# Leaving out the idle products of TensorE in the later stages of a one-core attention and expert kernel

## The chip, the cores and the metric

The kernel runs on one core of one Trainium2 chip. The metric is the device time of one execution in microseconds (us), lower is better. The times below are medians over separate executions; the profile is one further execution, taken by the hardware profiler.

## What is computed

One transformer layer on `x` of 1 x 256 x 512 (256 tokens, width 512), float32, in three steps, each a layer norm followed by a block whose result is added to `x`:

```
x = x + xattn(norm(x), ctx)     # 16 heads, 4096 context rows of width 128, rotary keys of width 64
x = x + attn(norm(x))           # causal latent attention, 16 heads, query/key width 96, value width 32
x = x + ffn(norm(x))            # 32 experts, 4 of them per token, capacity 10 tokens each, and a shared expert
```

The expert block: a router picks 4 of 32 experts for each token (first 3 of 8 groups, then 4 experts in them); each expert takes at most 10 tokens and computes `(silu(t @ W_gate) * (t @ W_up)) @ W_down` with 512 x 256, 512 x 256 and 256 x 512 weights; the results are weighted and added back to the tokens. A shared expert of inner width 512 is computed for all tokens.

## The kernel before

The program is written by hand for each engine, with semaphores. Each engine works through its own list in order. TensorE (PE) runs: a preparation stage (to about 60 us), the cross attention in 8 pairs of heads (to about 450 us), its output projection (to about 500 us), the second attention (`queries`, `scores2`, `transposes2`, `values2`, to about 546 us), the projection of its output into `x2_banks` (line 1287), the transposes of the normed tokens `xn_transposes(3)` (line 992), the router's logits (line 1295), and then the expert stage.

The expert stage, in TensorE's order: `shared_hidden(0)` (line 1307), which is the first quarter of the shared expert's hidden layer; the positions of the chosen tokens (lines 1324 to 1326), for which VectorE must have chosen the experts (`sel_done`); `chosen_rows(c)` (line 1335), which gathers the tokens of all experts by a product with a one-hot matrix that VectorE makes from the positions (`oh_done`); then eight groups of four experts, g = 0 to 7. For each group `gate_up(g, c)` runs for four quarters c of the width (line 1363), ScalarE and VectorE make silu(gate) * up, `hidden_back(g)` transposes it (line 1376), ScalarE copies it back, and `down(g)` (line 1397) multiplies by the down weights. Between them stand the other quarters of the shared expert, its output `shared_out` (line 1316) and `combine` (line 1406), which adds the experts' results into two accumulation banks. The last group has its down product in two halves n = 0, 1 of the output width, each followed by a copy on VectorE and `combine_last(n)` (line 1413); VectorE then adds to `x` (line 974) and two stores write the output.

The expert weights are 48 MB, 1.5 MB for an expert, and stream through a ring of 13 places of on-chip memory. SyncE (SP) issues the loads in a fixed order. Places 0 to 11 are filled before or during the second attention. The others are loaded when TensorE is through with what lay there: quarter by quarter for the first two groups (semaphore `gu_part`), then by expert. The last three experts (k = 29, 30, 31) are loaded last of all: their gate and up weights in four quarters (`ld_end_gu[c]`), then the down weights of group 7's first expert (k = 28), then the down weights of the last three in two halves (`ld_end_down[n]`, line 414). `down(6)` needs the down weights of k = 24 to 27; `down(7)` half n needs k = 28 and `ld_end_down[n]`.

TensorE's clock is granted at one of two levels. The kernel holds runs of idle products, made by `warm(n, bank)` at line 981: n products of a 128 x 128 by 128 x 512 bf16 matrix of constants into a bank whose content nobody reads. They compute nothing of the result. They stand in TensorE's list, so that work behind them waits for them.

Of the kernel before, what the change touches and what calls it, by code (L numbers as in the profile page):

```python
# [43 lines left out]
NG = E // GE  # L44
# [55 lines left out]
DVE_BEFORE = order("rows0 q0 rows1 rope0 rows2 q1 k0 rows3 q2 rope1 m0 k1 rope2 rope3 k2 m1 m2 q3 k3 m3 m4 m5 q4 k4 m6 m7 m8 q5 "  # L100
                   "k5 m9 m10 k6 m11 m12 q6 m13 k7 m14 m15 q7")
PAIR_BUFS = 6
WARM_START, WARM_HEADS, WARM_TURN, WARM_LAST, WARM_QUARTER, WARM_DOWN, WARM_CHOICE, WARM_ROWS = 14, 3, 4, 9, 3, 6, 3, 4


def expert(k):
# [12 lines left out]
def wait(eng, sem, value):  # L119

    if isinstance(value, int) and value <= 0:
        return
    eng.wait_ge(sem, value)
# [12 lines left out]
def layer(nc, a, out):  # L136
    with ExitStack() as ctx:
# [3 lines left out]
        def ps(name, cols):  # L141
            return ctx.enter_context(nc.psum_tensor(name, [P, cols], F32))
# [112 lines left out]
        psM = ps("psM", 1024)  # L255
        psA = [psM[:, 0:512], psM[:, 512:1024]]
        psE = [psS[0][:, 0:512], psS[0][:, 512:1024]]
        psF = [psS[1][:, 0:512], psS[1][:, 512:1024]]
# [719 lines left out]
        def _(pe):  # L978
            mm = nc.tensor.matmul

            def warm(n, bank, of=const[:, C_EARLY:C_EARLY + 256].bitcast(BF16)):

                for _ in range(n):
                    mm(bank[:, 0:512], of[:, 0:P], of[:, 0:512], start=True, stop=True)  # L984
# [3 lines left out]
            def xn_transposed(n, s):  # L988
                for c in range(DC):
                    if c % 2 == 0:  # L990
                        pe.wait_ge(ln_xn, 2 * (TT * (n - 1) + s) + c // 2 + 1)
                    last = nc.tensor.transpose(psE[s][:, P * c:P * c + P], xn[:, s, P * c:P * c + P], ident)
                last.then_inc(ln_tr, 1)

            def xn_transposes(n):
                for s in range(TT):
                    xn_transposed(n, s)
                    if n == 3 and s == 0:
                        warm(WARM_LAST, psF[1])

            def rope_transposes(n):
                pe.wait_ge(kr_done, n + 1)
# [178 lines left out]
            for h in range(H + 2):  # L1181
# [6 lines left out]
                if 1 <= h <= H:  # L1188
                    g = h - 1
# [31 lines left out]
            def values():  # L1221
                for st in range(TT):
                    mm(psF[st][:, :], ckv[:, P * st:P * st + P], w_vb, start=True, stop=True).then_inc(v_mm, 1)

            def queries(h):

                if h == 0:
                    pe.wait_ge(ld_qb, 16)
                if h % 4 == 0:
                    wait(pe, qk_copied, h)  # L1230
                    w = slice(NOPE * h, NOPE * (h + 4))
                    mm(psA[1][:, 0:T], w_qn[:, w], qa, start=True, stop=True)
                    mm(psA[1][:, T:2 * T], w_kn[:, w], ckv, start=True, stop=True).then_inc(nope_mm, 1)
                wait(pe, q2_turned, 2 * h - 2)
                mm(psE[h % 2][:, 0:T], w_qb[:, h, :], qa, start=True, stop=True).then_inc(q2_mm, 1)

            def scores2(h):
                if h == 0:
                    pe.wait_ge(kpe_spread, 1)
                    pe.wait_ge(v_copied, TT)  # L1240
                pe.wait_ge(q2_done, h + 1)
                pe.wait_ge(qk_copied, h + 1)
                wait(pe, s2_max, h - 1)
                q, k = qk[0:QW, h % QK_BUFS, 0:T], qk[0:QW, h % QK_BUFS, T:2 * T]
                mm(psF[h % 2][:, 0:P], q[:, 0:P], k[:, 0:P], start=True, stop=True)
                mm(psF[h % 2][:, P:3 * P], q[:, P:T], k, start=True, stop=True).then_inc(s2_mm, 1)

            def transposes2(h):
                pe.wait_ge(s2_exp, 2 * h + 2)
                wait(pe, pT_copied, h if h < NH2 - 1 else 0)  # L1250
                if h == NH2 - 1:
                    pe.wait_ge(qk_copied, NH2)
                for i in range(3):
                    last = nc.tensor.transpose(turned_bank(h)[:, P * i:P * i + P], sm[:, h % SM_BUFS, P * i:P * i + P], ident)
                last.then_inc(pT_mm, 1)

            def values2(h):
                pe.wait_ge(pT_copied, h + 1)
                w = slice(V2 * h, V2 * h + V2)
                mm(psO[0][:, w], pT[:, h % 2, 0:P], v2[:, 0, w], start=True, stop=True)  # L1260
                mm(psO[1][:, w], pT[:, h % 2, P:2 * P], v2[:, 0, w], start=True, stop=False)
                mm(psO[1][:, w], pT[:, h % 2, 2 * P:3 * P], v2[:, 1, w], start=False, stop=True).then_inc(o2_mm, 1)
            for h in range(NH2 + 5):
                if h < NH2:
                    queries(h)
                if h == 0:
                    values()
                if h in (2, 3):
                    warm(WARM_HEADS, psM[:, 0:512])
                if 0 <= h - 1 < NH2:  # L1270
                    scores2(h - 1)
                if 0 <= h - 3 < NH2:
                    transposes2(h - 3)
                if 0 <= h - 4 < NH2:
                    values2(h - 4)
            warm(WARM_TURN, psF[1])
            for st in range(TT):
                pe.wait_ge(o2_done, st + 1)
                for c in range(DC):
# [20 lines left out]
            def shared_hidden(i):  # L1300
                if i == 0:
                    pe.wait_ge(ld_shared[0], 16)
                elif i == DC - 1:
                    pe.wait_ge(sh_done, 2)
                for n in range(2):
                    for c in range(DC):
                        last = mm(sh_bank[i][:, T * n:T * n + T], sh_in[:, i, n, c, :], xnT[:, c, :], start=c == 0, stop=c == DC - 1)  # L1307
                last.then_inc(sh_mm, 1)
# [7 lines left out]
                        mm(psO[n][:, D // 2 * st:D // 2 * (st + 1)], hs[:, i, P * st:P * st + P], sd[:, i, halves[n]],  # L1316
                           start=i == 0 and st == 0, stop=False, skip_group_check=True)
            shared_hidden(0)
            warm(WARM_CHOICE, psF[1])
            pe.wait_ge(sel_done, 1)  # L1320
            pe.wait_ge(ld_const, 32)
            early, ones = const[:, C_EARLY:C_EARLY + P], const[:, C_ONES:C_ONES + P]
# [1 line left out]
            mm(psA[1][:, 0:E], early, chosen[:, 0, :], start=True, stop=True)  # L1324
            mm(psA[1][:, E:2 * E], ones, chosen[:, 0, :], start=True, stop=False)
            mm(psA[1][:, E:2 * E], early, chosen[:, 1, :], start=False, stop=True).then_inc(pos_mm, 1)
            warm(WARM_ROWS, psF[1])
            pe.wait_ge(cleared, 2)

            def chosen_rows(c):  # L1330
# [7 lines left out]
            def weights_by_slot():  # L1338
                pe.wait_ge(ow_done, 2 * TT)
                pe.wait_ge(hT_copied, 2)  # L1340
                for trio in range(TRIOS):
                    for st in range(TT):
                        o = T * trio + P * st
                        last = nc.tensor.transpose(psS[0][:, o:o + P], ow[:, st, P * trio:P * trio + P], ident)
                last.then_inc(back_mm, 1)
# [33 lines left out]
            def down(g):  # L1379
                trio = g // 3  # L1380
                pe.wait_ge(hT_copied, g + 1)
                wait(pe, y_copied, min(trio, TRIOS - 1))
                for j in range(GE):
                    k = GE * g + j
                    if k < ENDING:
                        pe.wait_ge(ld_down[k % RING], 16 * (k // RING + 1))
                for n in range(2 if trio == TRIOS - 1 else 1):
                    if g == NG - 1 or g == NG - 2 and n == 0:
                        warm(WARM_DOWN, psF[0])
                    if g == NG - 1:  # L1390
                        pe.wait_ge(ld_end_down[n], 16 * (E - ENDING))
                    bank, out = (psA[n], slice(D // 2 * n, D // 2 * (n + 1))) if trio == TRIOS - 1 else (psA[trio % 2], slice(0, D))
                    for c in range(FC):
                        for j in range(GE):
                            k = GE * g + j
                            o = W_GU + D * c
                            last = mm(bank[SLOT * j:SLOT * j + SLOT, out], hT[:, g % 3, c, SLOT * j:SLOT * j + SLOT], ring[k % RING][:, o + out.start:o + out.stop],  # L1397
                                      start=g % 3 == 0 and c == 0, stop=(g % 3 == 2 or g == NG - 1) and c == FC - 1, skip_group_check=True)
                    if n == 1 or trio < TRIOS - 1 or g == NG - 1:
                        last.then_inc(y_mm, 1)  # L1400
# [29 lines left out]
            shared_hidden(2)  # L1430
            for g in range(2, NG):
                for c in range(DC):
                    if g == NG - 1:
                        warm(WARM_QUARTER, psF[0])
                    gate_up(g, c)
                if g == 2:
                    shared_hidden(3)
                    weights_by_slot()
                elif g < 3 + DC:
                    shared_out(g - 3)  # L1440
                if g == NG - 1:
                    down(g - 1)
                hidden_back(g)
                if g == 3:
                    combine(0)
                elif g == 6:
                    combine(1)
                if g != NG - 2:
                    down(g)
# [82 lines left out]
```

## Time and profile before

| | |
|---|---|
| median of 3 runs | 666.23 us (666.22 to 668.37) |
| profiled execution, its own time | 665.71 us |
| profiled execution, span of the instructions | 663.5 us |
| mean granted clock of TensorE in it | 0.995 |
| TensorE busy | 627.0 us (94%) |
| VectorE (DVE) / ScalarE (ACT) / GpSimd (POOL) busy | 389.3 / 363.0 / 178.1 us |
| read from device memory | 77.29 MB |

Times in the trace count from the span's start. The profiled execution's own time is 2.2 us above its span, and lies 0.5 us below the median. A row of the timeline gives start, duration, engine, line of the kernel, operation, output and inputs with their shapes, the number of instructions merged, and in square brackets how long the engine had been idle before and what released it. One float32 product appears as two instructions. Ends of matmuls are modelled, so that the last one of a row reaches a little into the next row, and a few records are missing. A granted clock of 1.00 is the upper level, 2.4 GHz; 0.50 is the lower, 1.2 GHz.

### The profile page before, as it was taken

To read this page: it belongs to the slowest core of one execution; us is meant where nothing else is said; L and a number is where in the kernel's file an instruction comes from. 1 tells how busy PE (TensorE), PEld (TensorE's weight loads), DVE (VectorE), ACT (ScalarE), POOL (GpSimd) and SP (SyncE) were. 2 spreads that over 40 slices of the span, in tenths; PEclk is the share of its full clock that TensorE was granted. 3 is DMA by queue.
4 is the path that set the end of the run, shared out by engine and by line. 5 is a ranking of instruction groups with operands and counts; after the bars stand their busy time and mean duration, and the time that the engine had idled before them with its cause. 6 is when DMAs were issued, how large, how long until landed. Compare 5 with 4: busy or idle time off the path is not lost.

```text
span 663.5 us, 15252 instructions
## 1 busy us (share of the span) xinstructions
PE 627.0 (94%) x5998; PEld 463.3 (70%) x6054; DVE 389.3 (59%) x549; ACT 363.0 (55%) x518; POOL 178.1 (27%) x143
## 2 busy tenths in 40 slices
PE   8999899999999999999999999999998999995997
PEld 5876766777777777777777778997556986361443
DVE  5979586767766766766766766553145865300001
ACT  4442765766776776776776777784126874100000
POOL 1260334444443443453453443000001320000000
PEclk9999999999999999999999999999999999997999
DMA  9953874224224224224224224204986043699993
GB/s 351 419 166 79 239 271 96 56 55 98 53 53 95 53 53 95 53 53 95 53 53 95 55 54 105 46 2 192 420 354 255 1 159 128 215 393 414 417 393 101
DMA packets 32152, 105.15 MB, mean 158 GB/s; under 512 B 4592, under 2 KB 9968, under 8 KB 27760
## 3 DMA queue, kind: packets, MB, share of 16 engines
q1 hardware_dynamic: 32112, 104.57, 49.6%
q8 instruction: 30, 0.49, 0.3%
q14 instruction: 10, 0.08, 0.0%
HBM read 77.29 MB, written 0.52 MB: 117 GB/s over the span
## 4 chain that ended last, share of the span: by engine, by line
PE 75%; DVE 9%; issue 6%; ACT 5%; DMA 3%; SPq 1%; POOL 1%; DVEq 0%; ACTq 0%
PE psO L1115 8%; PE psO L1124 8%; PE psO L1116 8%; PE psS L1102 7%; PE psS L1103 7%; PE psM L1074 5%; PE psS L1363 5%; PE psO L1180 4%; DMA arena<-rope 3%; PE psO L1059 3%; DVE arena L768 2%; PE psM L1397 2%; PE psO L1060 2%; PE psO L1307 2%; PE psS L984 1%
## 5 line engine op out<-in xcount | busy, mean ns | idle before, releaser
L768 DVE TENSOR_REDUCE arena<-psM 128x2 f32<-128x1024 f32 x121 | 147.7, 1221 | 66.6 <-PE psM L1074 66.2
L589 ACT ACTIVATE arena<-psS 128x1024 bf16<-128x1024 f32 x128 | 131.3, 1026 | 88.9 <-PE psS L1103 86.8
L484 POOL TENSOR_TENSOR arena<-arena 128x1024 bf16<-128x1024 f32 x56 | 120.8, 2156 | 190.4 <-ACT arena L590 166.9
L1115 PE MATMUL psO<-arena 128*128 128x129 bf16 x1024 | 132.8, 220 | 1.5 <-ACT arena L589 1.2
L1116 PE MATMUL psO<-arena 128*128 128x128 bf16 x1024 | 132.4, 220 | 0.0
L590 ACT ACTIVATE arena<-psS 128x1024 f32<-128x1024 f32 x128 | 130.9, 1023 | 0.0
L1102 PE MATMUL psS<-arena 128*128 128x256 bf16 x512 | 120.5, 273 | 0.9 <-DVE arena L779 0.9
L1103 PE MATMUL psS<-arena 65*128 65x256 bf16 x512 | 120.8, 273 | 0.0
L1115 PEld LDWEIGHTS psO<-arena 128*128 128x128 bf16 x1024 | 99.1, 98 | 20.3 <-issue 12.7
L1116 PEld LDWEIGHTS psO<-arena 128*128 128x128 bf16 x1024 | 99.4, 97 | 6.7
L806 DVE TENSOR_TENSOR arena<-arena 128x1024 bf16<-128x1024 f32 x72 | 88.6, 1233 | 14.6 <-ACT arena L590 14.6
L1124 PE MATMUL psO<-arena 128*128 128x129 bf16 x1024 | 79.4, 220 | 0.7 <-DVE arena L806 0.5
L1124 PEld LDWEIGHTS psO<-arena 128*128 128x128 bf16 x1024 | 65.8, 97 | 3.5 <-DVE arena L806 1.8
L1102 PEld LDWEIGHTS psS<-arena 128*128 128x128 bf16 x512 | 50.2, 98 | 7.4 <-DVE arena L701 1.0
L1103 PEld LDWEIGHTS psS<-arena 65*128 65x128 bf16 x512 | 50.0, 98 | 5.4
L581 ACT CAST arena<-psO 128x512 bf16<-128x512 f32 x64 | 37.8, 591 | 26.6 <-PE psO L1060 26.6
L762 DVE TENSOR_TENSOR arena<-psO,arena 128x512 bf16<-128x512 f32 x64 | 43.8, 684 | 12.1 <-ACT arena L581 11.4
L1074 PE MATMUL psM<-arena 64*128 64x512 bf16 x242 | 47.1, 386 | 3.7 <-DVE arena L768 2.8
L1363 PE MATMUL psS<-arena 128*32 128x512 f32 x256 | 32.5, 638 | 5.8 <-issue 5.8
L960 DVE TENSOR_TENSOR arena<-psS,arena 128x256 f32<-128x256 f32 x8 | 3.4, 424 | 55.0 <-ACT arena L666 55.0
L1059 PE MATMUL psO<-arena 128*128 128x512 bf16 x64 | 24.3, 379 | 8.0 <-issue 7.5
L527 POOL TENSOR_TENSOR arena<-arena 64x256 f32<-64x256 f32 x16 | 11.5, 718 | 72.5 <-DVE arena L849 72.5
(197 smaller groups left out, 739.2 us busy)
## 6 DMA issues: line engine op xcount, KB each, us to landing
arena<-arena SPq DMA_DIRECT2D x96, 256.0 KB, 3.7
arena<-w_exp SPq DMA_DIRECT2D x20, 1024.0 KB, 16.0
arena<-w_exp SPq DMA_DIRECT2D x29, 512.0 KB, 13.4
arena<-w_exp SPq DMA_DIRECT2D x54, 256.0 KB, 8.1
arena<-w_pair SPq DMA_DIRECT2D x8, 1088.0 KB, 19.2
arena<-w_o SPq DMA_DIRECT2D x1, 4096.0 KB, 20.3
arena<-ctx SPq DMA_DIRECT2D x4, 512.0 KB, 12.8
arena<-rope SPq DMA_DIRECT2D x4, 512.0 KB, 14.1
```

Source lines behind the costliest of these rows:

```text
L484: nc.gpsimd.tensor_tensor(p_lo[:, s % 2, :], p_f[:, s % 2, :], p_hi[:, s % 2, :], ALU.subtract).then_inc(s_plo[0], 1)
L589: nc.scalar.activation(p_hi[:, s % 2, :], psS[s % 2][:, :], ACT.Exp).then_inc(s_phi, 1)
L590: nc.scalar.activation(p_f[:, s % 2, :], psS[s % 2][:, :], ACT.Exp).then_inc(s_pf, 1)
L768: nc.vector.reduce_max(maxes[:, :, st, c], maxima_bank(q, m)[:, :].rearrange("p (j n) -> p j n", j=2), AX.X).then_inc(s_mfree, 1)
L806: nc.vector.tensor_tensor(p_lo[:, s % 2, :], p_f[:, s % 2, :], p_hi[:, s % 2, :], ALU.subtract).then_inc(s_plo[s % 2], 1)
L1074: last = mm(bank[:, 512 * j:512 * j + 512], queries_of[r, P * st:P * st + P], k_hi[r, 512 * c:512 * c + 512], start=True, stop=True)
L1102: mm(o, k1[:, j, l], q1[:, j, :], start=True, stop=False)
L1103: last = mm(o, k2[0:R + 1, j, l], q2[0:R + 1, j, :], start=False, stop=True)
L1115: mm(psC[:, st, :], ph, vx[:, GROUP * g + i, 0:CW], start=g == 0 and i == 0 and st == 0, stop=False, skip_group_check=True)
L1116: last = mm(psC[:, st, 0:K], ph, vx[:, GROUP * g + i, CW:VW], start=False, stop=False, skip_group_check=True)
L1124: last = mm(psC[:, st, :], p_lo[:, s % 2, T * i + P * st:T * i + P * st + P], vx[:, GROUP * g + i, 0:CW], start=False, stop=g == HALF - 1 ...
L1363: last = mm(psF[g % 2][SLOT * j:SLOT * j + SLOT, :], xpT[:, c, CAP * e:CAP * e + SLOT], ring[k % RING][:, 2 * FI * c:2 * FI * (c + 1)], st ...
```

## The change

Of the eight constants that give the lengths of the idle runs only `WARM_START` (14 products in the first microseconds) is left; the seven others and their calls are deleted. That takes out of TensorE's list: 3 products each in the rounds h = 2 and 3 of the second attention, 4 after it, 9 between the two tiles' transposes of the third layer norm, 3 before the wait for the chosen experts, 4 after the positions, 3 before each of the four quarters of `gate_up(7, c)`, and 6 each before `down(6)`, `down(7)` half 0 and `down(7)` half 1. In all 56 products. Nothing is added or moved.

```
-WARM_START, WARM_HEADS, WARM_TURN, WARM_LAST, WARM_QUARTER, WARM_DOWN, WARM_CHOICE, WARM_ROWS = 14, 3, 4, 9, 3, 6, 3, 4
+WARM_START = 14
...
                     xn_transposed(n, s)
-                    if n == 3 and s == 0:
-                        warm(WARM_LAST, psF[1])
...
-                if h in (2, 3):
-                    warm(WARM_HEADS, psM[:, 0:512])
                 if 0 <= h - 1 < NH2:
                     scores2(h - 1)
...
-            warm(WARM_TURN, psF[1])
             for st in range(TT):
                 pe.wait_ge(o2_done, st + 1)
...
             shared_hidden(0)
-            warm(WARM_CHOICE, psF[1])
             pe.wait_ge(sel_done, 1)
...
-            warm(WARM_ROWS, psF[1])
             pe.wait_ge(cleared, 2)
...
                 for n in range(2 if trio == TRIOS - 1 else 1):
-                    if g == NG - 1 or g == NG - 2 and n == 0:
-                        warm(WARM_DOWN, psF[0])
                     if g == NG - 1:
                         pe.wait_ge(ld_end_down[n], 16 * (E - ENDING))
...
                 for c in range(DC):
-                    if g == NG - 1:
-                        warm(WARM_QUARTER, psF[0])
                     gate_up(g, c)
```

## Rows read from the trace of the kernel before

**Rows 1.** The page: granted clock and memory traffic, 40 equal slices of 16.6 us.
```profile
PEclk9999999999999999999999999999999999997999
GB/s 351 419 166 79 239 271 96 56 55 98 53 53 95 53 53 95 53 53 95 53 53 95 55 54 105 46 2 192 420 354 255 1 159 128 215 393 414 417 393 101
```

**Rows 2.** Timeline of TensorE after its longest idle time, and one group later.
```profile
607.77 6.10 PE L1363 MATMUL psS<-arena 128*32 128x512 f32 x32 [5.82 <-issue]
...
619.41 3.62 PE L1363 MATMUL psS<-arena 128*32 128x512 f32 x32
```

**Rows 3.** Timeline of all engines in the last 24 us.
```profile
640.64 1.89 PE L1406 MATMUL psO<-arena 128*128 128x256 f32 x8
...
643.11 1.06 PE L1363 MATMUL psS<-arena 128*32 128x512 f32 x8
...
649.90 0.42 DVE L960 TENSOR_TENSOR arena<-psS,arena 128x256 f32<-128x256 f32 x1 [10.34 <-ACT arena L666]
...
650.75 1.93 PE L1397 MATMUL psM<-arena 128*32 128x256 f32 x32
...
652.62 0.44 PE L1376 MATMUL psS<-arena 128*128 128x128 f32 x2
653.09 0.23 ACT L674 COPY arena<-psS 128x80 f32<-128x80 f32 x1 [3.22 <-PE psS L1376]
...
654.77 1.07 PE L1397 MATMUL psM<-arena 128*32 128x256 f32 x16
...
657.17 1.07 PE L1397 MATMUL psM<-arena 128*32 128x256 f32 x16
...
658.17 1.99 PE L1413 MATMUL psO<-arena 128*128 128x256 f32 x8
```

**Rows 4.** Two of the last loads: SP's issue, then KB and us from issue to landing.
```profile
637.52 2.81 SPq L414 DMA_DIRECT2D arena<-w_exp  x1
arena<-w_exp SPq DMA_DIRECT2D x1, 256.0 KB, 12.9
...
645.01 0.59 SPq L414 DMA_DIRECT2D arena<-w_exp  x1
arena<-w_exp SPq DMA_DIRECT2D x1, 256.0 KB, 7.4
```

**Rows 5.** Timeline of all engines, from the second attention's end to the logits.
```profile
545.95 1.29 DVE L875 TENSOR_TENSOR arena<-psO,arena 128x512 f32<-128x512 f32 x2 [1.75 <-PE psO L1262]
...
546.70 1.25 PE L1280 MATMUL psS<-arena 128*128 128x128 f32 x8
...
555.52 2.11 PE L984 MATMUL psS<-arena 128*128 128x512 bf16 x9
...
557.95 0.76 PE L992 MATMUL psS<-arena 128*128 128x128 f32 x4 [0.32 <-DVE arena L722]
```

**Rows 6.** Timeline of all engines, from the shared product to the gather.
```profile
560.29 3.70 PE L1307 MATMUL psS<-arena 128*128 128x256 f32 x16
...
564.99 0.41 PE L1324 MATMUL psM<-arena 128*128 128x32 f32 x2 [0.35 <-DVE arena L897]
...
565.98 0.89 DVE L933 TENSOR_TENSOR arena<-psM,arena 128x320 f32<-128x320 f32 x2 [0.33 <-PE psM L1326]
...
566.62 2.39 PE L1335 MATMUL psS<-arena 128*128 128x320 f32 x8
```

**Rows 7.** Timeline of all engines, start of the second attention.
```profile
509.91 0.30 PEld L1245 LDWEIGHTS psS<-arena 96*128 96x128 f32 x2 [0.61 <-POOL arena L527]
...
511.91 0.70 PE L1232 MATMUL psM<-arena 128*128 128x256 f32 x2 [0.75 <-ACT arena L630]
```

**Rows 8.** Windows: PE, PEld, DVE, ACT, POOL busy (instructions), granted clock, DMA share, GB/s.
```profile
598.00:600.00 2.00, 0.73 (x5) 0.28 (x3) 0.42 (x1) 1.11 (x3) 0.00 (x0) 1.00 1.03 412
...
605.50:606.00 0.50, 0.00 (x0) 0.00 (x0) 0.00 (x0) 0.00 (x0) 0.00 (x0) 0.94 1.06 397
...
612.50:613.00 0.50, 0.50 (x8) 0.14 (x4) 0.00 (x0) 0.00 (x0) 0.00 (x0) 0.73 0.99 410
```

More of the change, by code:

```diff
@@ L102 @@
 PAIR_BUFS = 6
-WARM_START, WARM_HEADS, WARM_TURN, WARM_LAST, WARM_QUARTER, WARM_DOWN, WARM_CHOICE, WARM_ROWS = 14, 3, 4, 9, 3, 6, 3, 4
+WARM_START = 14
 def expert(k):
@@ L997, in xn_transposes @@
                     xn_transposed(n, s)
-                    if n == 3 and s == 0:
-                        warm(WARM_LAST, psF[1])
             def rope_transposes(n):
@@ L1267, in _ @@
                     values()
-                if h in (2, 3):
-                    warm(WARM_HEADS, psM[:, 0:512])
                 if 0 <= h - 1 < NH2:
@@ L1275, in _ @@
                     values2(h - 4)
-            warm(WARM_TURN, psF[1])
             for st in range(TT):
@@ L1318, in _ @@
             shared_hidden(0)
-            warm(WARM_CHOICE, psF[1])
             pe.wait_ge(sel_done, 1)
@@ L1326, in _ @@
             mm(psA[1][:, E:2 * E], early, chosen[:, 1, :], start=False, stop=True).then_inc(pos_mm, 1)
-            warm(WARM_ROWS, psF[1])
             pe.wait_ge(cleared, 2)
@@ L1387, in down @@
                 for n in range(2 if trio == TRIOS - 1 else 1):
-                    if g == NG - 1 or g == NG - 2 and n == 0:
-                        warm(WARM_DOWN, psF[0])
                     if g == NG - 1:
@@ L1432, in _ @@
                 for c in range(DC):
-                    if g == NG - 1:
-                        warm(WARM_QUARTER, psF[0])
                     gate_up(g, c)
```

## The prediction

> **What bounds the kernel now.** I started with the page's slices [rows 1]. The clock is full throughout except near 605 us, and from 580 to 647 us memory traffic is at about 400 GB/s: the expert weights stream without a pause. Next, in the timeline of that stretch, I asked who waits for whom. TensorE waits 5.82 us for weights up to 607.77 [rows 2]; from there its work follows on to the end with waits of about half a microsecond at most. So in the last 56 us TensorE's own list sets the end, and the loads run ahead of it. The last look was at how far ahead: the last load, a piece of the second half of the last down weights, is issued at 645.01 and lands 7.4 us later, at 652.4; the product that needs it starts at 657.17 [rows 4, 3]. TensorE is 4.75 us late for its last weights. That distance decides this change, because the idle products of the last group lie in TensorE's list with no wait beside them that would cover them.
>
> The earlier idle products act on the end in another way. The weight stream restarts only when TensorE is through the first quarter products (about 570 us), and from 577 on the channel is full. A shift of TensorE's work before 570 shifts the whole stream, the end of the wait at 607.77 and the last landing by the same amount.
>
> **The change part by part.** 56 products go. A run of nine takes 2.1 us [rows 5]; below, pairs of starts give the cost of each run.
>
> *The last group (30 products).* Before, `gate_up(7)` starts at 643.11 and `down(6)` at 650.75, with three runs of 3 between the quarters and one of 6 behind: 7.64 us [rows 3]. The same 32 instructions take group 4, which has no idle products, 3.62 us [rows 2]. That part would shrink by 4.0 us. The run ahead of the first quarter reaches from the end of `combine`, 640.64 + 1.89 less the 0.07 by which a row's modelled end overlaps the next row (657.17 + 1.07 against 658.17), to 643.11: 0.65 us. The run before half 0 of `down(7)` reaches from the end of ScalarE's copy, 653.32, to 654.77: 1.4 us. Half 0 then takes 1.0 and half 1 starts at 657.17: another 1.4 us [rows 3]. TensorE's list loses 4.0 + 0.65 + 1.4 + 1.4 = 7.45 us.
>
> The end does not gain all of that, because the weights are late next. I follow the list without idle products. `gate_up(7)` runs from 642.46 to 646.08. `down(6)` takes 1.87 (650.75 to 652.62), to 647.95; VectorE's silu product of group 7 was ready 1.0 us after the last quarter (650.32 against 649.35) and is still covered by it. The transposes and ScalarE's copy take 0.7 (652.62 to 653.32), to about 648.7. Half 0 needs the load issued at 637.52 and landed 12.9 us later, at 650.4 [rows 4]: a wait of 1.7, which also hides a wait of `down(6)` for its own last weights. Half 0 ends at 651.4. Half 1 needs the last landing, 652.4, another wait of 1.0. The rest (half 1, `combine_last`, VectorE's add, the stores) follows half 1 as before. Gain: 657.17 - 652.4 = **4.75 us**. The other 2.7 us turn into waits for weights.
>
> *The runs of the routing stretch (9 + 3 + 4).* After the 9 products TensorE still waited 0.32 us for VectorE's norm (L722) [rows 5], after the 3 it waited 0.35 us for the chosen experts (L897) [rows 6]: both runs lie beside VectorE's work, gain 0. After the 4 the gather starts at 566.62. VectorE's two one-hot products take 0.89 us from 565.98: the first is there at 566.42, the second at 566.87 [rows 6]. The gather's second pair of instructions could start at about 567.0 where it started at 567.15: gain 0.15.
>
> *The 4 after the attention.* VectorE's first scaling ends at 545.95 + 0.65 = 546.6, the transposes start at 546.70 [rows 5]: gain 0.05.
>
> *The 3 + 3 in the attention.* About 0.65 us each, by the run ahead of the first quarter. Behind the second run TensorE waited for GpSimd's add, and at 511.91 it waits 0.75 us for ScalarE [rows 7]. Gain 0 therefore; the upper bound is 0.65, were TensorE to pace that stretch, the lower is nothing, since nothing there waits longer without them.
>
> Sum: 4.75 + 0.15 + 0.05 = 4.95 us. The profiled execution would take 665.71 - 4.95 = 660.8; the median lies 0.5 above it, so **661.3 us**, 0.74% faster.
>
> **What the clock may take back.** The idle products kept TensorE busy over stretches that now have holes, and the trace of before cannot show what the clock does there. It shows one fall. TensorE was idle from 601.95 to 607.77; the clock went to the lower level, 1.2 GHz, at about 606, after 4 us of idleness, and was back at 2.4 GHz at about 612.7, after 5 us of dense work [rows 8, 2]. The 32 instructions in it took 6.10 us where 3.62 are usual: 2.5 us is the price of one fall over dense work [rows 2]. The new holes are 2.4 us (555.5 to 557.95), 1.0 (to 564.99) and 0.6 in the routing stretch, and 1.7 and 1.0 at the end. All are shorter than the idleness that preceded the fall, and from 598 to 600 TensorE worked 0.73 of 2 us at full clock [rows 8]. So the main sum takes 0 for the clock (the bounds: 0, and both rivals below together, 5.4), and falls are priced as rivals. The fall at 606 itself stays; with TensorE 1.0 us early for its last weights, one costlier by up to 1.0 would be hidden.
>
> The Trainium skill, "TensorE: Matmul & The Clock Gate", section "A second HAM failure mode: psum-queue depth-cycling", says that many short pauses between groups of matmuls can be enough to make the clock go back and forth. By it the first two rivals would hold, one or both. No row here shows a fall of that kind.
>
> **The rivals.**
> *One: the clock falls in the routing stretch.* For it: the 2.4 us hole is followed by products with very small outputs and then by further holes. Against: none is as long as 5.82 us. Price: 2.5 us of slower dense work, mostly the shared product (3.70 us) [rows 6]. Up to 0.95 is hidden in the wait for the chosen experts, and up to 1.9 more is lost if the logits, for which VectorE waits, take twice their 1.9 us: 1.5 to 4.4, taken 2.5. The stream starts that much later: 663.8.
> *Two: the clock falls at the very end.* From 648.7 to 652.4 TensorE would work only 1.0 us. Price: half 1 and `combine_last`, 1.0 + 1.9 us, double [rows 3]: 2.9 us, 664.2. With the first together: 666.7, no change.
> *Three: the loads do not hold TensorE up.* If the last landings came earlier, all 7.45 + 0.2 us would come out: 658.6. Against: the channel is full up to then.
> *Four, the other side: the clock falls in the routing stretch and stays low through it.* From 558 to 570 TensorE has about 10 us of work ahead of the stream's start; all of it at 1.2 GHz adds up to 10, less the 0.95 hidden: 9 us, 670.3. This is slower than before by over 0.5% from a delay of 4.95 + 3.3 = 8.3 us on. Against: the one fall seen ended after 5 us of dense work.
> *Five: the products were free and the change does nothing.* That needs a last landing at 657. Against: traffic falls to a quarter of its rate in the last slice [rows 1].
>
> **How the numbers follow.** The forecast, clock held: 0.44. Fall in the routing stretch alone: 0.22. At the end alone: 0.14. Both: 0.08. Loads not binding: 0.05. Low throughout: 0.05. Products free: 0.02. 0.5% (3.3 us) is about what a measurement of this kernel tells from no change, so faster means below 662.9. The forecast, the third rival and a quarter of the first (its cheap end is 662.8) give 0.44 + 0.05 + 0.06 = 0.55 faster; slower are the fourth rival and a costly case of both falls, 0.07; 0.38 lie within. The range: 1.0 below the sum, for loads that land a little earlier and for the 0.65 of the attention, gives 660.3 and leaves out the third rival; the upper end, 666.7, takes in both falls. The forecast's own range is 660.3 to 662.3.
>
> **What would show it.** In the profile after: no idle products behind 7 us; TensorE's wait ahead of group 3 still some 5.8 us and the last landing near 652; waits for loads of about 1.7 us before half 0 (or shared with `down(6)`) and 1.0 before half 1, and half 1 starting 4.8 us earlier. The granted clock from 555 to 570 and beyond 648 says which rival holds; a shared product (line 1307) of clearly more than 3.7 us is the sign of the first. The prediction is wrong if the last landing has moved later by more than a microsecond, by whatever cause, or if a fall of the clock stands before the stream's start or behind the last landing.

## The result and the profile after

The changed kernel takes 664.34 us (median of 20 executions, 663.29 to 669.12) where the kernel before, run beside it, takes 667.16 us (20 executions, 665.79 to 670.37). The ratio is 0.9963, with a 95% interval from 0.9948 to 0.9978: 2.5 us faster by the ratio (the two medians lie 2.8 us apart), half of what was forecast (4.95 us, 0.74%). The profiled execution has a span of 662.1 us against 663.5, 1.4 us less, and a mean granted clock of 0.987 against 0.995.

The page's slices, granted clock and memory traffic, answer to [rows 1]:

```profile
PEclk9999999999999999999999999999999998898999
GB/s 349 419 167 80 224 290 96 56 55 98 53 53 95 53 53 95 53 53 95 53 53 95 55 54 97 54 2 165 419 361 279 1 133 154 105 381 407 417 402 226
```

Two things moved. The clock is now also low ahead of the weight stream, and the traffic begins later (133, 154 and 105 GB/s in the slices ahead of the full stream, where 159, 128 and 215 stood) and ends later (226 in the last slice, 101 before).

The windows show where the clock changed (PE, PEld, DVE, ACT, POOL busy with instructions, granted clock, DMA share, GB/s):

```profile
547.00:547.50 0.50, 0.50 (x5) 0.33 (x5) 0.35 (x1) 0.00 (x0) 0.00 (x0) 0.88 1.05 442
550.50:551.00 0.50, 0.50 (x2) 0.14 (x1) 0.00 (x0) 0.00 (x0) 0.00 (x0) 0.70 0.12 49
561.00:561.50 0.50, 0.50 (x5) 0.50 (x4) 0.00 (x0) 0.50 (x1) 0.00 (x0) 0.54 0.00 0
567.50:568.00 0.50, 0.50 (x3) 0.42 (x2) 0.01 (x1) 0.00 (x0) 0.00 (x0) 0.64 0.00 0
```

There are two new falls to 1.2 GHz: from about 547.4 to 550.8, and from about 561.0 to 567.9 (a row's granted clock is the mean over its half microsecond, so that 0.88 puts the fall 0.38 us into it). Between the four rows all windows have 0.50 within a fall and 1.00 outside. The timeline, answering to [rows 5] and [rows 6] (the code has lost some lines: L1275 was L1280, L1282 L1287, L1290 L1295, L1302 L1307, L1328 L1335):

```profile
546.81 1.71 PE L1275 MATMUL psS<-arena 128*128 128x128 f32 x8 [0.85 <-DVE arena L875]
...
548.32 6.58 PE L1282 MATMUL psM<-arena 128*128 128x512 f32 x16
...
559.32 0.76 PE L992 MATMUL psS<-arena 128*128 128x128 f32 x4 [2.26 <-DVE arena L722]
...
559.92 2.54 PE L1290 MATMUL psM<-arena 128*128 128x32 f32 x16
...
562.27 6.46 PE L1302 MATMUL psS<-arena 128*128 128x256 f32 x16
...
570.09 2.39 PE L1328 MATMUL psS<-arena 128*128 128x320 f32 x8 [0.77 <-DVE arena L933]
```

The first fall came 0.6 us after the end of a hole of 0.85 us, the second 1.7 us after the end of the hole of 2.26 us, while TensorE was at work on the logits. What stands ahead of a fall need not be its cause; for the first it is at most a part of it, as the experiments show. The shared product takes 6.46 us instead of 3.70, and the gather starts at 570.09 instead of 566.62: 3.47 us later. The timeline of the end, answering to [rows 2] and [rows 3] (L1356 was L1363, L1388 L1397, L1369 L1376, L1404 L1413):

```profile
611.99 5.43 PE L1356 MATMUL psS<-arena 128*32 128x512 f32 x32 [6.57 <-issue]
...
646.01 3.64 PE L1356 MATMUL psS<-arena 128*32 128x512 f32 x32
650.32 1.93 PE L1388 MATMUL psM<-arena 128*32 128x256 f32 x32 [0.67 <-DMA arena<-w_exp]
652.18 0.44 PE L1369 MATMUL psS<-arena 128*128 128x128 f32 x2
653.88 1.07 PE L1388 MATMUL psM<-arena 128*32 128x256 f32 x16 [1.26 <-DMA arena<-w_exp]
655.74 1.07 PE L1388 MATMUL psM<-arena 128*32 128x256 f32 x16 [0.79 <-DMA arena<-w_exp]
656.75 1.99 PE L1404 MATMUL psO<-arena 128*128 128x256 f32 x8
```

Each down product of the end now waits for a load: 0.67, 1.26 and 0.79 us (some 0.3 us of the 1.26 is ScalarE's copy, which always stands there). The last load, in the same view as [rows 4]:

```profile
648.25 0.60 SPq L414 DMA_DIRECT2D arena<-w_exp  x1
arena<-w_exp SPq DMA_DIRECT2D x1, 256.0 KB, 7.5
```

It lands at 648.25 + 7.5 = 655.75, and half 1 starts at 655.74. It landed at 652.4 before: 3.35 us earlier. So the books of this pair of executions close: half 1 starts 657.17 - 655.74 = 1.43 us earlier, the span is 1.4 us shorter, and 4.75 less the stream's delay of 3.35 is 1.4.

### The profile page after: what moved, and what is told of

Read it like the earlier page. It is cut to its first block, busy times and chain, and to the rows that moved or that the text cites. A ratio compares the mean times of both kernels' runs of the same rounds, so it can differ in the third digit from the quotient of the medians.

```text
span 662.1 us, 15146 instructions
## 1 busy us (share of the span) xinstructions
PE 618.2 (93%) x5947; PEld 462.5 (70%) x5998; DVE 389.1 (59%) x549; ACT 363.0 (55%) x518; POOL 177.8 (27%) x143
## 4 chain that ended last, share of the span: by engine, by line
PE 71%; DVE 8%; issue 6%; ACT 5%; DMA 4%; SPq 4%; POOL 1%; DVEq 0%; ACTq 0%
PE psO L1113 8%; PE psO L1122 8%; PE psO L1114 8%; PE psS L1101 7%; PE psS L1100 7%; PE psM L1072 5%; PE psO L1178 4%; DMA arena<-rope 3%; PE psS L1356 3%; PE psO L1057 3%; DVE arena L768 2%; PE psO L1058 2%; PE psO L1302 2%; SPq L410 2%; PE psM L1388 1%
## 5 line engine op out<-in xcount | busy, mean ns | idle before, releaser
L1356 PE MATMUL psS<-arena 128*32 128x512 f32 x256 | 31.3, 625 | 6.6 <-issue 6.6
```

Source lines behind the costliest of these rows:

```text
L1356: last = mm(psF[g % 2][SLOT * j:SLOT * j + SLOT, :], xpT[:, c, CAP * e:CAP * e + SLOT], ring[k % RING][:, 2 * FI * c:2 * FI * (c + 1)], st ...
```

## The experiments

Each line below is one kernel, timed in rounds beside the kernel before on the same chip. "Clock" lists the mean granted clocks of its executions, lowest to highest; the kernel before had 0.987 to 0.995 in the 53 executions beside e, f and g, and medians of 667.26, 667.54 and 667.60 us. The profile of before, with the fall ahead of group 3 alone (605.9 to 612.8 us), has a mean of 0.995. "Off" and "kept" speak of the idle products; the constants stand in the order START, HEADS, TURN, LAST, QUARTER, DOWN, CHOICE, ROWS, and are 14, 3, 4, 9, 3, 6, 3, 4 in the kernel before.

| kernel | ratio, 95% interval | median us | clock |
|---|---|---|---|
| changed (all off but START) | 0.9963, 0.9948 to 0.9978 | 664.34 | 0.981 to 0.989 |
| e1: QUARTER, DOWN off | 0.9937, 0.9914 to 0.9959 | 662.95 | 0.985 to 0.995 |
| e2: HEADS, TURN, LAST, CHOICE, ROWS off | 1.0045, 1.0030 to 1.0060 | 670.15 | 0.984 to 0.987 |
| e3: TURN, LAST kept | 0.9942, 0.9921 to 0.9962 | 664.41 | 0.986 to 0.995 |
| e4: LAST kept | 0.9959, 0.9944 to 0.9974 | 663.96 | 0.984 to 0.991 |
| f1: before, and 24 more ahead of group 3 | 0.9968, 0.9953 to 0.9984 | 665.18 | 0.994 to 1.000 |
| f2: e1, and 24 more ahead of group 3 | 0.9937, 0.9918 to 0.9957 | 663.06 | 0.995 to 1.000 |
| f3: QUARTER off | 0.9955, 0.9937 to 0.9972 | 663.80 | 0.989 to 0.995 |
| f4: DOWN off | 0.9932, 0.9912 to 0.9951 | 662.42 | 0.990 to 0.995 |
| g1: e1, and 2 + 2 more in rounds 17 and 18 | 0.9916, 0.9897 to 0.9935 | 661.75 | 0.991 to 0.995 |
| g2: e1, and HEADS, TURN off | 0.9948, 0.9927 to 0.9969 | 664.08 | 0.984 to 0.992 |
| g3: CHOICE, ROWS kept | 0.9972, 0.9958 to 0.9987 | 665.59 | 0.984 to 0.989 |
| g4: LAST kept, and 2 + 2 more in rounds 17 and 18 | 0.9927, 0.9906 to 0.9947 | 662.67 | 0.989 to 0.995 |

### e1: only the last group's products off

```
-... = 14, 3, 4, 9, 3, 6, 3, 4
+... = 14, 3, 4, 9, 0, 0, 3, 4
```

(Here and below `...` stands for the eight names.)

> Only the 30 idle products of the last group go (three before each quarter, six before each down product); the 26 others stay. Theory A (the last group gains what was computed, and two falls of the clock ahead of the weight stream take part of it back): TensorE waits for the last weights, half 1 of the last down product starts about 4.75 us earlier, ratio 0.993, no fall of the clock between 540 and 570 us. Theory B (the last group was mis-sized and the early falls cost nothing at the end): the gain is that of the whole change, some 2.5 to 2.8 us, ratio 0.996.

Measured 0.9937, 4.2 us: nearer to theory A. The executions tell more than the median. Three of eight have a clock of 0.994 or 0.995, as much as the one fall ahead of group 3 gives; they take 660.99, 661.24 and 661.53 us. The kernel before, over the 53 executions that ran beside e, f and g, has 19 with such a clock, median 665.9 us. Like against like the last group gives 665.9 - 661.2 = 4.7 us, against 4.75 computed. The rest of e1's executions have a lower clock and take 662.7 to 667.1. The profile is one of those, and it contradicts the last clause of theory A: the clock fell ahead of the stream although all the early idle products are in place. A window, and the timeline around it:

```profile
546.50:547.00 0.50, 0.50 (x4) 0.50 (x4) 0.00 (x0) 0.00 (x0) 0.22 (x1) 0.60 0.72 262
```

```profile
545.37 0.55 PE L1254 MATMUL psM<-arena 128*128 128x128 f32 x3 [0.21 <-ACT arena L641]
...
546.20 0.39 PE L1262 MATMUL psO<-arena 128*128 128x32 f32 x2
546.49 0.56 PE L1260 MATMUL psO<-arena 128*128 128x32 f32 x2
...
547.71 1.89 PE L984 MATMUL psS<-arena 128*128 128x512 bf16 x4
```

There is no idle time over 0.21 us in this stretch; TensorE was busy with the transposes and 32-column products of the attention's last rounds when the clock fell at 546.6. The four idle products (L984) come after it and take 1.89 us for what takes 1.03 at full clock. This is not special to e1: with all 26 early products in place the profiles of f2, f3 and f4 have a fall there too (545.8 to 546.3), those of before and f1 have none.

### e2: only the early products off

```
-... = 14, 3, 4, 9, 3, 6, 3, 4
+... = 14, 0, 0, 0, 3, 6, 0, 0
```

> Only the 26 idle products ahead of the expert groups go; the 30 of the last group stay. Theory A: the clock falls near 547 and near 561 us as in the changed kernel, the gather starts about 3.5 us later, the weight stream and TensorE's list shift by it, and the kernel is slower than before by about 2.5 to 3.5 us, ratio 1.004 to 1.005. Theory B: the falls hide behind slack in the stream, ratio 1.000.

1.0045: 3.0 us slower, in the middle of what theory A gave, and theory B is out. All six executions have clocks of 0.987 or less. The early products are worth 3.0 us where TensorE's list sets the end. Between the changed kernel and e1 they are worth 1.7 us (0.9963 less 0.9937); the intervals of the two estimates overlap, so this is no evidence that they differ.

### e3 and e4: two runs, one run put back

```
-... = 14, 0, 0, 0, 0, 0, 0, 0
+... = 14, 0, 4, 9, 0, 0, 0, 0        (e3)
+... = 14, 0, 0, 9, 0, 0, 0, 0        (e4)
```

> The changed kernel with two runs put back: the 4 products after the attention and the 9 between the transposes. Theory A: these two cover the holes of 0.85 and 2.26 us, ahead of which the clock fell; it stays up, the gather starts near 566.6 us, the time is that of the kernel with only the last group's products gone, ratio 0.993. Rival (the small holes matter too, those beside the chosen experts and in the attention's first rounds): a fall stays somewhere between 500 and 570 us, ratio 0.995 to 0.997.

> The changed kernel with only the 9 products between the transposes put back. If each fall belongs to the hole next to it: the fall near 547 us stays and costs 1.3 us, the one near 561 us is gone, ratio 0.995. If the second fall is caused by the long hole and the first is chance: no fall in most runs, ratio 0.993. If the 9 products are not what holds the clock: both falls stay, ratio 0.996.

e3 gave 0.9942, e4 0.9959; their intervals overlap each other and those of e1 and of the changed kernel, so the ratios decide little. The clocks decide more: with the nine products in place e4's median clock is 0.989 where the changed kernel's is 0.986, and its profile has the fall near 547 and none near 561. In e3 two of six executions reach 0.995, at 661.48 and 661.51 us. Its profile has a fall at 546.7, with the 4 products after the attention in place, which is against theory A, and a later one, which the rival foretold, at 570.6, in the gather and behind holes of 1.00 and 0.77 us (timeline):

```profile
567.91 0.41 PE L1324 MATMUL psM<-arena 128*128 128x32 f32 x2 [1.00 <-DVE arena L897]
569.54 3.61 PE L1335 MATMUL psS<-arena 128*128 128x320 f32 x8 [0.77 <-DVE arena L933]
```

### f1 and f2: does TensorE's list or the last landing set the end?

```
                     if g == NG - 1:
                         warm(WARM_QUARTER, psF[0])
+                    if g == 3 and c == 0:
+                        warm(24, psF[1])
```

with the constants of the kernel before (f1) and of e1 (f2).

> The kernel before, with 24 more idle products in TensorE's longest wait, ahead of the first quarter of group 3 (5.2 us of them in a wait of 5.8 us or more). They hold the clock through that wait, so that the 32 instructions of group 3 take 3.6 us instead of 6.1 to 6.6. If TensorE's own list sets the end of the kernel before, the end gains 2.5 to 3 us, ratio 0.996. If the weights set it, nothing is gained, ratio 1.000.

> The same 24 products, and the 30 of the last group gone. If the last landing binds once the last group's products are gone, the fill gains nothing here: ratio 0.993 to 0.994, as without the fill (0.9937 measured), although the mean granted clock is higher by 0.005; the waits for weights in the last group are some 2.5 us longer. If TensorE's list still bound, the two gains would add up: ratio 0.990.

The timelines, first f1, then f2:

```profile
609.69 3.64 PE L1363 MATMUL psS<-arena 128*32 128x512 f32 x32 [2.32 <-issue]
```

```profile
610.79 3.64 PE L1363 MATMUL psS<-arena 128*32 128x512 f32 x32 [1.49 <-issue]
...
649.07 1.93 PE L1397 MATMUL psM<-arena 128*32 128x256 f32 x32 [2.40 <-DMA arena<-w_exp]
652.61 1.07 PE L1397 MATMUL psM<-arena 128*32 128x256 f32 x16 [1.23 <-DMA arena<-w_exp]
654.48 1.07 PE L1397 MATMUL psM<-arena 128*32 128x256 f32 x16 [0.80 <-DMA arena<-w_exp]
```

In both the fall ahead of group 3 is gone and the group takes 3.64 us. In the kernel before that is worth 2.1 us (0.9968); in e1 it is worth nothing (0.9937 with and without). The 2.4 us turn up ahead of `down(6)` as a wait for a load. So TensorE's list bound the kernel before, and the last landing binds it once the last group's products are gone, as the prediction had it. The 2.1 us rest on the medians; in the profiled execution of f1 the wait for weights ends at 609.69 us instead of 607.77, so that half 1 starts only 0.53 us earlier than in the profile of before (656.64 against 657.17). From the gather to the end of that wait the kept profiles differ by up to 1.8 us (41.15 in before, 42.94 in f1), and no run explains this. The idle products ahead of group 3, and the missing ones of group 7, pull at the same 4.75 us.

### f3 and f4: the two halves of the last group's products

```
-... = 14, 3, 4, 9, 3, 6, 3, 4
+... = 14, 3, 4, 9, 0, 6, 3, 4        (f3)
+... = 14, 3, 4, 9, 3, 0, 3, 4        (f4)
```

> Only the 12 idle products between the quarters of group 7 go. TensorE's list loses 12 x 0.217 = 2.6 us and is still behind the last landing: gain 2.6 us, ratio 0.996.

> Only the 18 idle products ahead of the last down products go. TensorE's list loses 18 x 0.22 = 4.0 to 4.2 us, just inside the distance of 4.75: gain 4.1 us, ratio 0.994, and a wait for a load of at most a few tenths. With the run between the quarters the two lists' losses sum to 6.7, and only 4.2 us were gained with both gone (0.9937): the difference is the wait for weights.

f3 gave 3.0 us (0.9955) for 2.6 expected, f4 4.5 us (0.9932) for 4.1, each within its interval. Their sum, 7.5 us, is about the 7.45 us that TensorE's list was computed to lose (the two intervals are about 1.2 us wide to each side); with both gone 4.2 us were measured. In other words f4's 18 products alone give as much as both, within the intervals.

### g1: idle products where the clock really fell

```
                 if 0 <= h - 4 < NH2:
                     values2(h - 4)
+                if h in (NH2 + 1, NH2 + 2):
+                    warm(2, psF[0])
```

with the constants of e1.

> The kernel with only the last group's 30 products gone, and 2 idle products added in each of the attention's rounds h = 17 and 18, where TensorE has only transposes and products of 32 columns between waits. The fall near 546 us, which came in about half of the executions of the kernel before too, is then gone if that stretch causes it: mean granted clock 0.995 in all executions, hardly any time above 662 us, median 661.5, ratio 0.991 to 0.992. If the fall has another cause, the clocks stay spread from 0.985 to 0.995, ratio 0.9937 or, as the four products delay the list, 0.994.

The timeline of g1 in that stretch:

```profile
543.86 0.38 PE L984 MATMUL psS<-arena 128*128 128x512 bf16 x1
...
545.08 0.59 PE L984 MATMUL psS<-arena 128*128 128x512 bf16 x2
...
546.09 1.03 PE L984 MATMUL psS<-arena 128*128 128x512 bf16 x4
547.11 1.25 PE L1282 MATMUL psS<-arena 128*128 128x128 f32 x8
548.53 3.67 PE L1289 MATMUL psM<-arena 128*128 128x512 f32 x8 [0.17 <-ACT arena L659]
```

0.9916 is the lowest ratio of all, though its interval overlaps that of e1; what sets g1 apart is the spread: six executions from 661.43 to 662.02 us, where e1's eight go from 660.99 to 667.14. Four of six clocks are 0.995. The four products delay the transposes by about 0.3 us (547.11 against 546.70, in a profile that already ran 0.15 later at 499 us) and, in this execution, no fall stands between 540 and 575 us. Its 661.75 us is near the 661.3 forecast for a kernel that holds the clock; but it keeps 26 idle products that the changed kernel lacks, and the kernel before took 667.60 beside it, not the 666.2 that the forecast started from, so the nearness is in part luck.

### g2, g3, g4: which of the runs hold the clock

```
+... = 14, 0, 0, 9, 0, 0, 3, 4        (g2)
+... = 14, 0, 0, 0, 0, 0, 3, 4        (g3)
+... = 14, 0, 0, 9, 0, 0, 0, 0        (g4, and the four lines of g1)
```

> The last group's 30 products, the 6 of the attention's first rounds and the 4 after it gone; the 9, 3 and 4 of the routing stretch stay. If the 4 after the attention hold the clock: the fall near 547 us is in all executions, ratio 0.995 to 0.996. If they do not (the fall came with them in place too): as with the last group's products alone gone, ratio 0.9937.

> The changed kernel with the 3 and 4 products beside the choice of experts put back, the 9 not. If the second fall (near 561 us) comes from the hole of 2.26 us that the 9 products covered, it stays, ratio 0.996 as in the changed kernel. If it comes from the small holes after it, it goes, ratio 0.994.

> The changed kernel with the 9 products put back and 2 idle products added in each of the rounds h = 17 and 18. If these two places are all that the clock needs ahead of the stream: no fall there in most executions, mean clock 0.995, ratio 0.992 with 17 idle products fewer than the kernel with only the last group's gone plus 4. If the small holes matter: clocks between 0.989 and 0.992 and ratio 0.994 to 0.995.

g2 gave 0.9948, between the two expectations, with a spread from 662.0 to 666.3 us. Its profile shows a fall that I had not looked for, in the attention's first rounds, where the products of HEADS stood (timeline, then window):

```profile
510.76 0.46 PE L1245 MATMUL psS<-arena 96*128 96x128 f32 x2 [1.39 <-ACT arena L630]
...
512.73 1.22 PE L1232 MATMUL psM<-arena 128*128 128x256 f32 x2 [0.75 <-ACT arena L630]
...
523.70 0.70 PE L1232 MATMUL psM<-arena 128*128 128x256 f32 x2 [0.16 <-ACT arena L630]
```

```profile
512.00:512.50 0.50, 0.00 (x0) 0.00 (x0) 0.47 (x2) 0.48 (x2) 0.50 (x1) 0.69 0.00 0
```

The same pair of instructions stands 10.97 us apart here and 9.56 in the kernel before (511.91 and 521.47, the first in [rows 7]): 1.4 us for that fall. It is the only one of seven kept profiles without the products of HEADS that has it. Whether the 4 products after the attention matter g2 does not tell: its profile has a fall at 549.7, but so have others, at 545.8 to 546.7, with those 4 in place. g3 (0.9972, no clock above 0.989) keeps the fall from 561 to 568 in its profile: it belongs to the long hole, not to the small ones. g4 (0.9927, clocks from 0.989 to 0.995) lies between its two expectations, nearer to the first. Its profile has the hole of 0.85 us ahead of the transposes, and no fall there; but one in the gather (567.6 to 571.0), as e3 had, and a third kind, the prediction's second rival: the clock falls at 653, among the waits for the last loads, and stays low to the end. Its windows and timeline:

```profile
567.50:568.00 0.50, 0.50 (x3) 0.37 (x2) 0.47 (x2) 0.00 (x0) 0.00 (x0) 0.63 0.00 0
...
652.00:653.00 1.00, 0.34 (x8) 0.00 (x0) 0.42 (x1) 0.00 (x0) 0.00 (x0) 0.98 0.14 48
```

```profile
651.27 1.07 PE L1399 MATMUL psM<-arena 128*32 128x256 f32 x16 [1.25 <-DMA arena<-w_exp]
...
653.88 1.93 PE L1399 MATMUL psM<-arena 128*32 128x256 f32 x16 [1.54 <-DMA arena<-w_exp]
...
655.75 3.78 PE L1415 MATMUL psO<-arena 128*128 128x256 f32 x8
```

Half 1 takes 1.93 us and `combine_last` 3.78 us, where 1.07 and 1.99 are usual: 2.7 us, against a forecast price of 2.9.

### Where the clock fell in the fourteen kept profiles

| fall | idle products that were or were not there | profiles with the fall |
|---|---|---|
| 545.8 to 549.7 us | neither the 4 after the attention nor those of rounds 17 and 18 | 5 of 5 (changed, e2, e4, g2, g3) |
| the same | the 4, not those of rounds 17 and 18 | 5 of 7 (e1, e3, f2, f3, f4; not before, f1) |
| the same | those of rounds 17 and 18 | 0 of 2 (g1, g4) |
| 561.0 to 562.9 us | the 9 between the transposes off | 3 of 3 (changed, e2, g3) |
| the same | the 9 kept | 0 of 11 |
| 567.6 or 570.6 us | the 9 kept, the 3 and 4 beside the choice of experts off | 2 of 3 (e3, g4; not e4) |
| the same | the 9 and the 3 and 4 kept | 0 of 8 |

So the 9 products did hold the clock at 561 us. The 4 after the attention did not reliably hold it at 546: the stretch of narrow products ahead of them has the fall with them and without them, and in e2 it came at 545.8, ahead of the hole that opens at 546.9. What removes it is work within that stretch, on two profiles and on the clocks and times of g1.

## Why the prediction was half right

**The last group: right.** The sum that TensorE's list loses, 7.45 us, is matched by f3 and f4 (3.0 + 4.5). That 4.75 of it count, and the rest turns into waits for weights, is shown twice: by f1 and f2, and by the executions of e1 with an undisturbed clock, 4.7 us faster than those of the kernel before. The three waits measured (0.67, 1.26, 0.79 us, sum 2.7) are those foretold (1.7 and 1.0, sum 2.7), one of them moved ahead of `down(6)`; without the copy's 0.3 us, which the prediction counted by itself, the match is within 0.3. The median of e1 gives 4.2 us, the 4.75 only its executions with an undisturbed clock.

**The runs ahead of the stream as work in TensorE's list: not contradicted.** After the attention and in the routing stretch TensorE waits for VectorE instead (0.85, 2.26, 0.77 us in the profile after), and at 512 us it is no earlier than before (512.02 against 511.91) and waits 0.75 us for ScalarE as before. The 0.2 us of the sum are too small to be seen in the times.

**The clock: wrong.** The step that failed is the sentence "So the main sum takes 0 for the clock". It rested on comparing the length of the new holes with the 4 us of idleness that preceded the one fall in the trace; its list of new holes also left out the one of 0.85 us behind the attention. The runs showed in its place that the early products held the clock for part of the time, and that with them gone it falls more often and for longer: the last group alone gave 4.2 us (e1), the whole change 2.5, so that the 26 early products are worth 1.7 us where the sum had a gain of 0.2 for leaving them out. The rest of the miss, some 0.5, is the 4.2 for 4.75. Long holes are not needed: the clock fell behind one of 2.26 us, behind 1.00 and 0.77, and in e1 with no idle time over 0.21 us, in a stretch of transposes and narrow products. All 20 executions of the changed kernel have a clock of 0.989 or less. In the profiled pair the falls cost 3.35 us at the last landing: at 559.32 TensorE is 1.37 us late (0.11 of it was there at 512), at the gather another 2.10 are added. The first rival had this mechanism at 2.5 us and a chance of 0.22; it was the rule, and a second fall stood ahead of it. By the prediction's own signs, a last landing over a microsecond later and a fall ahead of the stream's start, it was wrong. The Trainium skill's statement weighed there ("TensorE: Matmul & The Clock Gate", section "A second HAM failure mode: psum-queue depth-cycling": many short pauses between groups of matmuls can be enough) agrees with the row of e1 (no pause over 0.21 us), and I had given it too little.

**A second fault lay under it: the profile of before was one of its better executions.** The sum was made against an execution with a clock of 0.995 and 665.71 us. Of 53 later executions of that kernel 34 have a lower clock, median 667.9 us; 19 have 0.994 or 0.995, median 665.9. The idle products of the kernel before do not hold the clock either in most executions, and its trace showed one of those where they do. The mean clock does not say where a fall was: five kept profiles (e2, f2, f3, f4, g2) have one at 13.3 to 13.9 us, ahead of everything changed here, and in these the instruction that stands at 499.05 us in the profile of before starts at 499.6 to 499.9; it starts at 499.0 to 499.3 in the others, but for e1 and e3 (500.5, without such a fall). The base was low as well, 666.2 us assumed and 667.16 measured, 0.9 of the 3.0 us by which the forecast 661.3 misses 664.34; that 664.34 lies in the range given owes nothing to the sum.

**What stays open.** Why two executions of one kernel differ in the place of a fall: the span's start varies too (the same instruction ran at 499.05 in one profile and at 500.55 in another), and I did not vary it by itself. Of the seven kept profiles that have the 4 products after the attention and none in rounds 17 and 18, the two without the fall near 546 (before, f1) are the two that had come to this instruction earliest, at 499.05 and 499.17; this is a coincidence of seven cases, and no more is shown. The worth of HEADS alone was not measured; g2 removes it with TURN. The stretch at 546 us was filled in two kept profiles and twelve executions only.

## What to carry to other kernels

An idle product in the list of an engine that sets the end costs its full length, and is worth it only where the clock would fall in front of work that sets the end; here 30 products stood at the end, where they cost 4.2 us (in one kept profile of nine without them, that of g4, the clock fell in their place, for 2.7 us), and four more, put in at 544 us ahead of where the clock fell, narrowed the spread of the times from 6 us (eight executions of e1) to 0.6 (six of g1). Before pricing a removal, look at the times and the mean clocks of many executions, not at one trace: times that go with the value of the clock (665.9 us at 0.994 and 0.995, 667.9 below) say that the clock is already part of the time. A gain next to a stream of loads is cut off at the distance to the last landing: measure that distance first.

## What the runs showed of the hardware that was not expected

The granted clock fell to 1.2 GHz while TensorE's records show it busy: in e1 at 546.6, after five microseconds with no idle time over 0.21 us, in transposes of 128 x 128 and products of 32 columns. Two products of 512 columns put in at each of two places there (g1) left four of six executions with a mean clock of 0.995, that of the profile of before with its single fall. And the rise comes late: the changed kernel's clock stayed at 1.2 GHz from 561.0 to 567.9, with TensorE busy throughout, and the shared product took 6.46 us for 3.70.
